# A linear-attention and expert kernel: norms as products of squares, a query projection of split operands, and two waits taken in pieces

## What is computed

```python
x = x + layernorm(attn_block(layernorm(x)))      # linear attention, 16 heads of 16, 64 random features
x = x + layernorm(expert_block(layernorm(x)))    # 8 experts, each takes its top 512 rows

# inside attn_block
def softmax_kernel(x, proj, is_query):
    norm = x.shape[-1] ** (-0.25)
    xp = einsum('bhnd,md->bhnm', x * norm, proj)
    diag = sum(square(x), axis=-1, keepdims=True) * 0.5 * (norm * norm)
    stab = max(xp, axis=-1) if is_query else max(xp, axis=(-1, -2))
    return ratio * (exp(xp - diag - stab) + EPS_K)
qp, kp = softmax_kernel(q, proj, True), softmax_kernel(k, proj, False)
denom = einsum('bhnm,bhm->bhn', qp, kp.sum(2))
out = einsum('bhnm,bhmd->bhnd', qp, einsum('bhnm,bhnd->bhmd', kp, v)) / denom
x = layer_norm(video + out @ Wo.T + bo)
x = layer_norm(x + relu(x @ W1.T + b1) @ W2.T + b2)
```

## Time and profile before

| what | us |
|---|---|
| median of 3 runs | 795.41 (793.67 to 796.27) |
| the profiled execution | 794.28 |
| its span, first to last instruction | 792.5 |
| PE busy | 723.0 (91%) |
| DVE busy | 618.2 (78%) |
| ACT busy | 470.4 (59%) |
| POOL busy | 369.4 (47%) |
| PE's largest group, L2157, 448 records | 106.0 |

### The profile page before, as it was taken

How to read it: one execution, slowest core, us unless ns; L and a number is a source line. 1 busy time by engine, 2 the same in 40 slices (tenths; PEclk the granted TensorE clock), 3 DMA queues, 4 the chain that set the end, 5 groups by cost and what they waited for, 6 DMA issues and landing times. The chain is left out here.

```text
span 792.5 us, 16186 instructions
## 1 busy us (share of the span) xinstructions
PE 723.0 (91%) x6012; PEld 592.9 (75%) x6012; DVE 618.2 (78%) x1298; ACT 470.4 (59%) x749; POOL 369.4 (47%) x358
## 2 busy tenths in 40 slices
PE   8999999999999999999999979965899999999950
PEld 7867768768768768768768758865788889998850
DVE  5876678978888888888888787888858777777683
ACT  4645737867867867867857834464145544455470
POOL 4364306526527517517517512511337566445563
PEclk9999999999999999999999999999699999999985
DMA  8200010011011011011011011160246664556593
GB/s 244 39 2 2 1 54 2 27 54 56 28 54 54 26 53 54 26 53 54 26 53 29 29 54 55 55 196 0 73 176 167 160 151 93 129 153 167 124 271 116
DMA packets 51184, 62.60 MB, mean 79 GB/s; under 512 B 9408, under 2 KB 44992, under 8 KB 51136
## 3 DMA queue, kind: packets, MB, share of 16 engines
q1 hardware_dynamic: 44016, 49.74, 19.4%
q0 software_dynamic: 6864, 12.19, 8.1%
q10 hardware_dynamic: 256, 0.03, 0.0%
HBM read 40.85 MB, written 21.10 MB: 78 GB/s over the span
## 5 line engine op out<-in xcount | busy, mean ns | idle before, releaser
L2157 PE MATMUL pF<-w,h 128*128 128x256 f32 x448 | 106.0, 382 | 0.0
L2157 PEld LDWEIGHTS pF<-w,h 128*128 128x128 f32 x448 | 81.8, 190 | 13.1 <-issue 3.4
L1128 POOL DMA_INDIRECT kp<-row_scratch,idx_g x32 | 42.3, 1322 | 78.7 <-DVE idx_g L1829 54.8
L893 ACT ACTIVATE h<-pX,b1cur 128x512 f32<-128x512 f32 x64 | 44.1, 691 | 56.0 <-DVE b1cur L1929 41.9
L2588 PE MATMUL pX<-w_lo,h_hi 128*128 128x256 f32 x256 | 73.9, 289 | 0.8 <-issue 0.8
L982 POOL TENSOR_SCALAR ve<-mv 128x4 f32<-128x4 f32 x36 | 8.5, 236 | 141.5 <-DVE mv L1205 140.6
L2588 PE MATMUL pX<-w_hi,h_lo 128*128 128x256 f32 x256 | 72.4, 283 | 0.0
L2588 PE MATMUL pX<-w_hi,h_hi 128*128 128x256 f32 x256 | 72.4, 283 | 0.0
L1136 POOL DMA_INDIRECT acc_scratch<-qp,idx_s x28 | 54.7, 1955 | 21.5 <-DVE qp L1866 16.6
L1887 DVE TENSOR_TENSOR h_lo<-h,h_hi 128x512 fp32r<-128x512 f32 x64 | 42.8, 691 | 25.6 <-ACT h_hi L885 24.1
L1305 DVE RECIPROCAL den<-den 128x512 f32<-128x512 f32 x14 | 46.9, 3348 | 7.5 <-ACT den L541 7.5
(11 more groups left out here) (428 smaller groups left out, 2141.8 us busy)
## 6 DMA issues: line engine op xcount, KB each, us to landing
kp<-fc1T SPq DMA_DIRECT2D x8, 1024.0 KB
w<-fc2T SPq DMA_DIRECT2D x8, 1024.0 KB
xin<-video SPq DMA_DIRECT2D x7, 512.0 KB, 3.8
x<-video SPq DMA_DIRECT2D x7, 512.0 KB, 4.5
out<-x SPq DMA_DIRECT2D x7, 512.0 KB, 3.0
acc_scratch<-xf SPq DMA_DIRECT2D x7, 512.0 KB, 2.9
row_scratch<-y SPq DMA_DIRECT2D x7, 512.0 KB, 3.0
kp<-acc_scratch SPq DMA_DIRECT2D x4, 512.0 KB, 6.0
```

The source lines that it names most:

```text
L893: nc.scalar.activation(h[:, n, :], pM[n % M_SLOTS], ACT.Gelu_apprx_tanh, bias=b1cur[:, n:n + 1]).then_inc(he_ready, 1)
L1128: pool.indirect_dma_start(xg[:, g, :], None, row_d, bass.IndirectOffsetOnAxis(ap=idx_g[:, g:g + 1], axis=0)).then_inc(gathered, 16)
L2157: ins = nc.tensor.matmul(pF[m][:, half * D:(half + 1) * D], h[:, k, tok(2 * m + half)], w2[:, k, :], start=(k == 0), stop=(k == FC - 1))
```

## The change

The sums of squares become products on PE. For the keys ACT squares the transposed keys in one operation of SBUF (`k_squares`, 128x1024, behind the query copies); for the queries the squares `qsqT` are there already. `norms` on PE multiplies, for each of 4 token tiles and 2 halves, the squares as weights (128x128, float32) with a matrix of ones that has 8 columns: 8 instructions. The keys' product replaces `turn_heads`; the queries' is new and stands between `hidden(7)` and `ff_out(0, 0)`. DVE takes both from PSUM with one `tensor_scalar` of 128x64 each; `tops_with_norms` writes maximum and maximum plus norm side by side, so that one transpose carries both.

The query projection is done with split operands: `q_hi` (ACT, in place of `qsq_hi`), `q_lo` (DVE, in place of `qsq_lo`), `projbd_hi` and `projbd_lo` (built once). One selector product takes off maximum and norm together: five products become four, all float32r.

`context()` waits for each quarter of the keys' features as it reaches it, and one step of `ff_out(1, 0)` stands ahead of it, two stand behind `features_turned(1)`. `attention_out` starts on the first half of the heads when that is there, and waits four times. `turn_kmax` and `spread_kmax` move ahead by one `hidden` each. On DVE `k_top` moves between the first two query maxima, and `rest_of_queries` and the queries' norms stand behind the last two.

The core of the diff (the names `AX_X`, `TT`, `P` and so on as before; `of_16` is the matrix of ones by heads):

```diff
-(J_K, J_Q, J_V, J_DK, J_ST, J_CTX, J_KSUM, J_CTXT, J_DEN, J_OUT, J_WO) = (
-    0, 2, 4, 6, 8, 10, 11, 12, 13, 15, 17)
+(J_K, J_Q, J_V, J_DK, J_ST, J_DQ, J_CTX, J_KSUM, J_CTXT, J_DEN, J_OUT, J_WO) = (
+    0, 2, 4, 6, 7, 9, 10, 11, 12, 13, 15, 17)
...
-            def squares(i, m):
-
-                wait(act, dg_ready, i * 2 + m - 1)
-                take_a(i, J_DK + m, sq[:, m % 2].rearrange("p a b -> p (a b)"), ACT.Square, sq_ready)
+            def k_squares(i):
+
+                act.wait_ge(kT_ready, (i + 1) * G)
+                nc.scalar.activation(sq[:].rearrange("p a b d -> p (a b d)"), kT.rearrange("p g n -> p (g n)"), ACT.Square).then_inc(sq_ready, 1)
...
                 nc.scalar.activation(qsqT, qT[:], ACT.Square).then_inc(qsq_ready, 1)
-                act.wait_ge(qsq_ready, i * 2 + 1)
-                nc.scalar.activation(qsq_hi[:], qsqT, ACT.Copy).then_inc(qsq_ready, 1)
+                nc.scalar.activation(q_hi[:], qT[:], ACT.Copy).then_inc(qsq_ready, 1)
...
-            def norms(i, m, dg):
-                dve.wait_ge(sq_ready, i * 2 + m + 1)
-                nc.vector.tensor_reduce(dg[:, 2 * m:2 * m + 2, :], sq[:, m].rearrange("p a (h d) -> p a h d", d=DH), AX_X,
-                                        ALU.add).then_inc(dg_ready, 1)
+            def norms(i, job, dg):
+
+                dve.wait_ge(a_ready, i * A_JOBS + job + 1)
+                nc.vector.tensor_scalar(dg.rearrange("p t h -> p (t h)"), pA[job % 2][:, 0:TT * H], 0.5 * NORM * NORM, None, ALU.mult).then_inc(dg_ready, 1)
 
...
-            def rest_of_squares(i):
+            def rest_of_queries(i):
 
                 dve.wait_ge(qsq_ready, (i + 1) * 2)
-                nc.vector.tensor_tensor(qsq_lo[:], qsqT, qsq_hi[:].bitcast(F32), ALU.subtract).then_inc(ql_ready, 1)
+                nc.vector.tensor_tensor(q_lo[:], qT[:], q_hi[:].bitcast(F32), ALU.subtract).then_inc(ql_ready, 1)
...
-                nc.vector.tensor_tensor(mxT_lo[:], pXall[:, 0, :], mxT_hi[:].bitcast(F32), ALU.subtract).then_inc(ql_ready, 1)
+                nc.vector.scalar_tensor_tensor(out=mxT[:], in0=pXall[:, 0, :], scalar=rest_rows[:, 0:1], in1=mxT_hi[:].bitcast(F32),
+                                               op0=ALU.mult, op1=ALU.add).then_inc(ql_ready, 1)
...
+            def tops_with_norms(i):
+
+                dve.wait_ge(qmx_ready, i * Q_STEPS + TT)
+                dve.wait_ge(dg_ready, (i + 1) * 2)
+                tops, halves = (a.rearrange("p t (a r) -> p (t a) r", r=4).unsqueeze(2).to_broadcast([P, TT * 4, 2, 4]) for a in (mxq, dgq))
+                nc.vector.tensor_tensor(mxp.rearrange("p t (a x r) -> p (t a) x r", a=4, r=4)[:, :, 0:2], tops, halves,
+                                        ALU.add).then_inc(qmx_ready, 1)
...
-                    norms(i, 0, dgk)
-                    norms(i, 1, dgk)
                 if u is not None:
                     dve.wait_ge(za_ready, 2 * u + 2)
                     stats(3, su, z)
                 if i is not None:
                     k_max(i, 2)
                     k_max(i, 3)
-
+                    norms(i, J_DK, dgk[:])
                     dve.wait_ge(kmx_ready, (i + 1) * TT)
                     nc.vector.tensor_reduce(kmax[:], mxk[:].rearrange("p t h -> p h t"), AX_X, ALU.max).then_inc(kmax_ready, 1)
                     q_max(i, 0)
+                    k_top(i, sa)
                     q_max(i, 1)
-                    k_top(i, sa)
-                    rest_of_squares(i)
-                    dve.wait_ge(dg_ready, (i + 1) * 2)
+                    dve.wait_ge(dg_ready, i * 2 + 1)
                     k_shift(i)
                     k_sub(i, 0)
                     k_sub(i, 1)
                     q_max(i, 2)
                     q_max(i, 3)
+                    norms(i, J_DQ, dgq)
+                    tops_with_norms(i)
+                    rest_of_queries(i)
                     k_sub(i, 2)
                     k_sub(i, 3)
...
-            def turn_heads(i, m, src):
-                s = slot_a(i, J_DK + m)
-                for t2 in range(2):
+            def norms(i, job, squares):
+
+                s = slot_a(i, job)
+                for t in range(TT):
                     for g in range(G):
-                        cols = s[:, t2 * D:(t2 + 1) * D].rearrange("p (a g x) -> p g a x", a=4, g=G)[:, g]
-                        ins = turn(cols, src[:, g, tok(2 * (m % 2) + t2)])
+                        dst = s[:, t * H:(t + 1) * H].rearrange("p (a g k) -> p g a k", a=4, g=G)[:, g]
+                        ins = nc.tensor.matmul(dst, squares[:, g, tok(t)], of_16[:].rearrange("p (a k) -> p a k", a=4), start=True, stop=True)
                 ins.then_inc(a_ready, 1)
+
+            def norms_of_keys(i):
+                pe.wait_ge(sq_ready, i + 1)
+                norms(i, J_DK, sq[:].rearrange("p a b d -> p (a b d)").rearrange("p (g n) -> p g n", g=G))
+
+            def norms_of_queries(i):
+                pe.wait_ge(qsq_ready, i * 2 + 1)
+                norms(i, J_DQ, qsqT)
 
             def end_wo(m):
...
-                    if g == 0:
-                        pe.wait_ge(qsq_ready, (i + 1) * 2)
-                    parts = ((projbd[:], qT[:, g, :]), (selc[:].rearrange("p k m -> p (k m)"), qsq_hi[:, g, :]),
-                             (selc[:].rearrange("p k m -> p (k m)"), qsq_lo[:, g, :]),
-                             (selm[:, g].rearrange("p k m -> p (k m)"), mxT_hi[:]), (selm[:, g].rearrange("p k m -> p (k m)"), mxT_lo[:]))
+                    parts = ((projbd_lo[:], q_hi[:, g, :]), (projbd_hi[:], q_lo[:, g, :]), (projbd_hi[:], q_hi[:, g, :]),
+                             (selm[:, g].rearrange("p k m -> p (k m)"), mxT[:]))
                     for n, (w_, x_) in enumerate(parts):
                         for a in range(4):
                             rows = slice(32 * a, 32 * a + 32)
...
-                    pe.wait_ge(kp_ready, (i + 1) * TT)
                     pe.wait_ge(v_ready, (i + 1) * 2)
-                    first_batch(vsum_ready, 2)
                     s = slot_a(i, J_CTX)
                     steps = [(v[:, t], kp[:, t]) for t in range(TT)] + ([(vsum[:, 0:D], None)] if is_first(i) else [])
                     eps = epsk_c[:, 0:1].to_broadcast([P, P])
                     for g in range(G):
                         for t, (v_, k_) in enumerate(steps):
+                            if g == 0 and k_ is None:
+                                pe.wait_ge(vsum_ready, 2)
+                            elif g == 0:
+                                pe.wait_ge(kp_ready, i * TT + t + 1)
                             for q in range(4):
...
-                    pe.wait_ge(aT_ready, (i + 1) * C)
                     first_batch(wlo_ready, 4)
                     slots = [slot_a(i, J_WO + m) for m in range(2)]
-                    high, low = ((aT_hi, wo_lo), (aT_hi, wo_hi)), ((aT_lo, wo_hi),)
-                    for m in range(2):
-                        by_tokens(slots[m], high, 2 * m, True, False)
-                    pe.wait_ge(al_ready, (i + 1) * C)
-                    for m in range(2):
-                        by_tokens(slots[m], low, 2 * m, False, True)
-                    for m in range(2):
-                        by_tokens(slots[m], high + low, 2 * m + 1, True, True).then_inc(a_ready, 1)
+
+                    def part(t, k, a_, w_, start=False, stop=False):
+
+                        return nc.tensor.matmul(slots[t // 2][:, t % 2 * D:(t % 2 + 1) * D], a_[:, k, tok(t)], w_[:, k, :], start=start, stop=stop)
+
+                    first, second = (0, 2), (2, 0)
+                    for k in range(C):
+                        pe.wait_ge(aT_ready, i * C + k + 1)
+                        for t in first:
+                            part(t, k, aT_hi, wo_lo, start=k == 0)
+                            part(t, k, aT_hi, wo_hi)
+                        pe.wait_ge(al_ready, i * C + k + 1)
+                        for t in second:
+                            part(t, k, aT_lo, wo_hi, stop=k == C - 1)
+                    for t in (1, 3):
+                        for k in range(C):
+                            part(t, k, aT_hi, wo_lo, start=k == 0)
+                            part(t, k, aT_hi, wo_hi)
+                            ins = part(t, k, aT_lo, wo_hi, stop=k == C - 1)
+                        ins.then_inc(a_ready, 1)
 
                 def fold_of_values():
                     pe.wait_ge(wqkvo_in, 16 * 3)
...
                     features(i, J_XQ, qT, 0)
                 if ff:
                     hidden(4)
+                if att:
+                    turn_kmax()
+                if ff:
                     hidden(5)
                 if att:
-                    turn_kmax()
+                    spread_kmax()
                 if ff:
                     hidden(6)
                 if att:
                     features(i, J_XQ + 1, qT, 1)
-                    spread_kmax()
                 if ff:
                     hidden(7)
+                if att:
```

(33 more changed lines are left out.)

37 lines of the change are left out of this document (22 added, 15 removed).

## The result

The changed kernel takes 796.94 us (795.99 to 800.83, 12 runs), the kernel before 794.94 in the same comparison: ratio 1.0029, 95% interval 1.0016 to 1.0042. By the ratio it is slower by 2.3 us (the two medians differ by 2.0). The interval does not reach 1, but the difference is just inside the 2.4 that the prediction set as what can be told. The forecast added 3.3. The profiled execution took 795.99, its span is 794.2, 1.7 more than before.

What follows compares the result with a forecast made beforehand. PE, busy 91% of the span, sets the batches' pace. 7 x 0.91 = +6.4, attention -3.2, batch 1 -0.5, batch 0 +0.6 make +3.3 on 795.41, rounded 798.7 us; own range 796 to 802, whole range 794.5 to 803.5.

Steps and rivals of the forecast that it cites:

- the sum: Forecast terms added up for a steady batch: +0.91 us before attention_out's gain of 0.46, +0.45 in the table.
- Norms: Norm products on PE: 1.78 us each at 0.111 a record; keys +0.93 after the transposes go, queries +1.78 a batch.
- Projection: Query projection on PE: the float32 product goes, four float32r products stay; -0.96 us each half, -1.92 a batch.
- the one of context: PE's wait ahead of the context product, for the last quarter of the keys: goes, -0.28 us a batch.
- The new one at `turn_context`: New wait of PE at turn_context, ending with cs_copy: PE has 3.1 us, ACT needs 3.4; +0.3 a batch.
- Switches between tiled and full products: PE's changes between full and tiled work: one more change to tiled work and back, +0.1 us a batch.
- `attention_out`: Starting on the first half of the heads gains 0.46 us in batches 0 to 6, -3.2 in all; about 0.1 still waited.
- Batches 0 and 1: Batch 0, a chain over DVE and ACT: +0.6 us, from -1 to +2.5; batch 1 loses a values-copy wait: -0.5.
- narrow products below 0.1: Rival: norm records on PE run faster, at 0.08 us, costing 7.9 less: 790.8 us; chance 0.10.
- dip of the clock: Rival: the clock falls behind the new narrow products in every batch, 7 x 1.6 = 11 us: 810; chance 0.07.
- DVE against POOL: Rival: the second late k_sub reaches POOL's first add and they block each other; 0.6 us a batch, 803; chance 0.09.

Runs made afterwards that it cites:

- f2: Changed kernel with projbd_lo and two small constants allocated behind the others, so x2T_hi and the rest have the addresses of the kernel before: 805.87 us, 1.0153.
- g4: Kernel before with only its four ff_out steps in the three places of the changed kernel: 797.58 us, 1.0035.
- e2: Changed kernel with turn_kmax, spread_kmax and k_top back in the places of the kernel before: 803.52 us, 1.0101.
- e4: Kernel before with only attention_out in pieces, as in the changed kernel: 791.60 us, 0.9956.
- e3: Kernel before with only one unused tile of 576 bytes a partition ahead of selm, moving the buffers behind it: 791.56 us, 0.9952.
- f3: Changed kernel with the product of the queries' norms issued twice in batches 1 to 7: 830.16 us, 1.0446.
- e1: Changed kernel with the four ff_out steps back in one piece behind sums_of_keys: 800.69 us, 1.0071.
- f1: Changed kernel with the keys' norms as before (8 transposes, squares by ACT, sums on DVE), the queries' norms still a product: 805.77 us, 1.0152.
- g1: Kernel before with attention_out in pieces, a 576-byte unused tile ahead of selm, and context waiting for the keys by quarters: 788.46 us, 0.9908.
- g3: Kernel before with attention_out in pieces and an unused tile of 960 bytes ahead of selm: 791.78 us, 0.9953.

## Why the prediction was right

The direction was right, and so were most terms. That the size was right too (+2.3 measured, +3.3 forecast) is in part luck: two errors cancel each other. The steps of the change cost more than forecast, because the switches do; and the pace of products that no step touches rose, because operands moved. In the old places (f2) a batch is 59.92 long, +1.08, where the sum has +0.45.

- **Norms**: 1.81 and 1.70 a product, against 1.78. The record pace of the one row of this shape carried over: 0.113 and 0.106. This, +2.66 a batch, is the largest cost.
- **Projection**: -0.94 and -0.89 without the wait, against -0.96.
- **Waits**: the one of context went. The new one at `turn_context` did not come: I put 3.1 us of PE against 3.4 of ACT. ACT took its 3.4 (`cs_copy` ended at 280.21), but PE took 280.26 - 276.80 = 3.46, because the steps in pieces cost more than the 0.1 I gave them. Cost moved from the wait to the switches.
- **Switches between tiled and full products**: the term that was mis-sized. The sum has 0.1; the four steps in pieces cost 0.56 (g4: 0.54). `spread_kmax` between two full products costs about 0.4 more than in its old place (7.58 against e2's 7.15), which I had at nothing, at most 0.1. 0.46 + 0.43 more for switches and 0.3 less for the wait make 0.6, the difference between 1.08 and 0.45.
- **`attention_out`**: -0.44 against -0.46; alone it is worth 3.5 us (e4), forecast 3.2. About 0.2 is still lost ahead of the first low part (292.86 to 293.17 in batch 4 of the changed kernel, where its neighbours follow at 0.12); I had put 0.1.
- **Batches 0 and 1**: forecast +0.6 and -0.5. Batch 0 ended 0.70 earlier (62.62 against 63.32), since `attention_out` began 1.7 earlier there, a gain that I did not count for batch 0's longer wait; batch 1 was the same within 0.04.
- **Pace by address**: not foreseen; the three constants pushed x2T_hi 576 bytes on. Worth 3.8 us by e3's ratio, 3.9 by f2's stretches. Without it the change by its own steps costs about 2.3 + 3.8 = 6 us, an estimate, and the forecast of 3.3 would have been little more than half of that.
- **Rivals**: no narrow products below 0.1. No dip of the clock in the batches of the profiled execution, but its 12 runs spread from 796 to 801 with mean clocks of 0.971 to 0.961, and f3 and e2 show such dips behind narrow products. Whether those slower runs had them there is not shown. DVE against POOL was 0.55 us away. (The add at 268.30 that I read as ending just after POOL's, 270.01, ended at 271.10: it stood until POOL was done and then ran for its own 1.1.) I gave each under a tenth; of the five variants of this kernel (e1, e2, f1, f2, f3) three had both within the batches.

## What to carry to other kernels

Before reading a difference of half a per cent as the work of an edit, compare the pace of a product that it did not touch: a constant of some hundred bytes moved a tile and gave 0.5%. On an engine that is always busy, count each switch between tiled and full products (0.14 to 0.2 us here) and each narrow record at its pace (0.11 us here), not at its columns. A wait that has gone is worth nothing until the next ones, the exponential's and POOL's in g1, are shown to be out of the way. And when an operation leaves or joins a queue, look at what the other engines then run at the same time: a sum of squares on DVE moved a POOL add onto an operation of 16x16, and PE paid 1.4 us.

## What was not expected of the hardware

- 512-column float32r products followed each other at 0.2333 or 0.2271 us, depending only on where the operands lie in SBUF (e3, f2), at the same granted clock; in one more place (g3) it was 0.2325.
- After 3.9 us of transposes, features and norms the granted clock was 0.50 for 3.4 us in one batch of e2, and late in or right behind the doubled norms (3.5 to 3.9 us) in six batches of f3, for up to 7 us; the same code in other batches kept 1.00.
- Two `k_sub` of 128x1024 took 4.53 instead of 2.35 us beside a POOL add of the same size (e2), and a DVE operation of 16x16 took 2.37 instead of 0.22 when it began with such an add (f1).
